# Key-value sums of the linear attention as plain float32 matmuls in four 32-column strips

## The reference, cut to what matters

```python
k = (key @ Wk.T + bk), v = (value @ Wv.T + bv)          # split into 16 heads of 16
k_prime = relu(einsum('bhnd,fd->bhnf', k, Wkf)) * attention_mask[:, None, :, None]
kv = einsum('bhnf,bhne->bhfe', k_prime, v)              # 64 x 16 for each head
qkv = einsum('bhmf,bhfe->bhme', q_prime, kv)
k_sum = sum(k_prime, axis=2)
qk_sum = einsum('bhmf,bhf->bhm', q_prime, k_sum)[..., None]
out = qkv / (qk_sum + 1e-08)
```

## Time and profile before

| | |
|---|---|
| median of 3 runs | 1415.89 us |
| profiled execution, span | 1415.0 us |
| PE busy over the span | 1280.9 us (91%) |
| weight loads busy | 1117.0 us (79%) |
| DVE / ACT / POOL busy | 1013.9 / 839.4 / 538.6 us |
| `key_value_sums`, first DMA issue to last copy | 906.02 to 1258.15 us |
| `linear_readout` | 1266.9 to about 1307.2 us |

### The profile page before, as it was taken

The page is one execution under the profiler, slowest core; times in us unless marked ns, Lnnn a source line. Parts: engine busy times, 40 slices in busy tenths (PEclk is TensorE's granted clock), DMA queues, the critical chain, the costliest instruction groups (busy, mean ns, idle before and its releaser), DMA issues. The chain is left out here.

```text
span 1415.0 us, 24244 instructions
## 1 busy us (share of the span) xinstructions
PE 1280.9 (91%) x7718; PEld 1117.0 (79%) x7718; DVE 1013.9 (72%) x2103; ACT 839.4 (59%) x1448; POOL 538.6 (38%) x551
## 2 busy tenths in 40 slices
PE   4679999999999999999996779699999999978797
PEld 3448888888888878888885768589999999965686
DVE  5857878887788887778865853488888888865533
ACT  4737667565666757666652244277777778742442
POOL 2646363644536354463522424121212121220342
PEclk9859999999999999999997889899999999989799
DMA  4031111010111101010003200211111010005000
GB/s 145 2 86 45 45 44 45 28 60 0 43 43 43 43 20 67 1 43 0 1 1 118 95 1 0 79 42 34 44 29 43 29 43 29 0 13 192 1 1 14
DMA packets 34188, 57.06 MB, mean 40 GB/s; under 512 B 2791, under 2 KB 29780, under 8 KB 33620
## 3 DMA queue, kind: packets, MB, share of 16 engines
q1 hardware_dynamic: 34132, 56.35, 12.2%
HBM read 55.89 MB, written 0.46 MB: 40 GB/s over the span
## 5 line engine op out<-in xcount | busy, mean ns | idle before, releaser
L716 POOL TENSOR_TENSOR att_sq<-att_work,att_sq 128x500 fp32r<-128x500 f32 x96 | 127.1, 1324 | 178.5 <-DVE att_sq L614 178.5
L721 POOL TENSOR_TENSOR att_k<-att_work,att_k 128x500 fp32r<-128x500 f32 x96 | 129.7, 1351 | 159.6 <-DVE att_k L622 159.6
L103 PE MATMUL att_csum<-att_pT,att_cn 125*128 125x448 f32 x384 | 155.3, 404 | 1.3 <-DVE att_pT L660 0.4
L538 ACT ACTIVATE att_pr<-att_pr,att_nmx 112x1500 f32<-112x1500 f32 (+1 forms) x96 | 108.6, 1131 | 68.1 <-DVE att_nmx L651 68.1
L105 PE MATMUL att_csum<-att_pT,att_cn 125*128 125x448 f32 x384 | 140.1, 365 | 0.0
L104 PE MATMUL att_csum<-att_pT,att_cn 125*128 125x448 f32 x384 | 139.6, 363 | 0.0
L1428 DVE SCALAR_TENSOR_TENSOR kvs_kp<-kvs_feat,kvs_kp 125x512 fp32r<-125x512 f32 x192 | 123.3, 684 | 18.4 <-ACT kvs_kp L1379 18.4
L1379 ACT ACTIVATE kvs_kp<-kvs_feat,kvs_zero 125x512 fp32r<-125x512 f32 x192 | 121.7, 685 | 23.0 <-PE kvs_feat L1312 21.4
L660 DVE TENSOR_TENSOR att_pT<-att_ring,att_pT 125x448 fp32r<-125x448 f32 x192 | 118.5, 617 | 23.1 <-ACT att_pT L554 22.8
L648 DVE TENSOR_SCALAR_CACHE_REDUCE att_pr<-att_ring 112x500 f32<-112x500 f32 x192 | 120.9, 675 | 4.4 <-PE att_ring L105 2.6
L527 ACT ACTIVATE att_work<-att_proj,att_eps 128x500 f32<-128x500 f32 x96 | 64.8, 675 | 97.0 <-PE att_proj L105 97.0
(11 more groups left out here) (256 smaller groups left out, 3486.2 us busy)
## 6 DMA issues: line engine op xcount, KB each, us to landing
att_raw_n<-in_ctx SPq DMA_DIRECT2D x16, 750.0 KB
kvs_raw<-in_ctxT SPq DMA_DIRECT2D x24, 500.0 KB, 3.6
attention_raw_t<-in_ctxT SPq DMA_DIRECT2D x7, 1500.0 KB, 6.3
w_gate<-in_gate SPq DMA_DIRECT2D x1, 2112.0 KB, 8.2
w_up<-in_up SPq DMA_DIRECT2D x1, 2112.0 KB, 12.8
qry_raw<-in_wq SPq DMA_DIRECT2D x4, 512.0 KB, 5.3
wo_raw<-in_wo SPq DMA_DIRECT2D x4, 512.0 KB, 6.3
w_down<-in_down SPq DMA_DIRECT2D x1, 2048.0 KB, 18.1
```

Of the source, the lines that this page charges most:

```text
L103: nc.tensor.matmul(out, w_lo, x_hi, start=start, stop=False, skip_group_check=True)
L716: nc.gpsimd.tensor_tensor(sq[1][:, i % 2, :], work[:, i % 2, :], sq[0][:, i % 2, :].bitcast(F32), ALU.subtract).then_inc(sq_lo, 1)
L721: nc.gpsimd.tensor_tensor(k[1][x], work[:, i % 2, :], k[0][x].bitcast(F32), ALU.subtract).then_inc(k_lo, 1)
```

## The change

The sums become plain float32 matmuls, one for each block and head (16 for each block instead of 12). The stationary operand is the 125 x 17 slice of `vs` (16 masked values of one head and the mask), the moving operand the 64 features of the same head. Head h writes to the partitions 32j to 32j+16 of one PSUM bank, j = 0 to 3, so four heads lie in four 32-column strips of the array, and the inner loop goes over the strips. `vs` and `kp` hold all 12 blocks of a batch (float32, not split), so `add` runs once a chunk over its 4 blocks, behind the first block of the next chunk.

With that, ACT and DVE share the features: ACT makes the lower half, DVE the upper half, both straight from `feat`, one instruction each for a block. The values are masked by one DVE instruction from `vals_ps` (two buffers now); the bias is no longer added there but, times the mask sum, once a batch in `read_blocks`. At the end of a batch ACT copies four strips (17 x 256 each) to SBUF, PE turns them with two 128 x 128 transposes (`turn`), and DVE writes the blocks of `kvd` with 6 instructions (`read_blocks`), in the stretch of the next batch's first chunk. `linear_readout` finds `kvd` ready: `turn_sums`, `take_low` and `diagonal` are gone, and its loop is `read`, divide, turn. `kvd` for all batches is zeroed by POOL in a block of its own ahead of `key_value_sums`.

```diff
+            def add(b, c):
+                n = b * KT + (c + 1) * TPC
+                wait(pe, v_set, n)
+                wait(pe, v_mask, n)
+                wait(pe, kp_low, n)
+                wait(pe, kp_high, n)
+                if c == 0:
+                    wait(pe, kv_taken, 4 * b)
+                for t in range(c * TPC, (c + 1) * TPC):
+                    for r in range(4):
+                        for j in range(4):
+                            h = 8 * (r // 2) + 2 * j + r % 2
+                            last = nc.tensor.matmul(sums[32 * j:32 * j + RV, r * FD:(r + 1) * FD], vs[:, t, h, :],
+                                                    kp[:, t, h * FD:(h + 1) * FD], start=(t == 0 and r == 0),
+                                                    stop=(t == KT - 1 and r == 3), skip_group_check=True)
                 last.then_inc(sums_done, 1)
+            def turn(b):
+                wait(pe, kv_taken, 4 * (b + 1))
+                wait(pe, kvd_done, 4 * b)
+                for a in range(2):
+                    last = nc.tensor.transpose(turned[:, a * 128:(a + 1) * 128], kv[:, a * 128:(a + 1) * 128], ident[:])
+                last.then_inc(kv_turned, 1)
...
+                for c, project, _ in chunks(b, last):
+                    for i in range(TPC):
+                        values(b, c * TPC + i)
+                        features(b, c * TPC + i)
+                        if i == 0:
+                            if c > 0:
+                                add(b, c - 1)
+                            elif not first:
+                                add(b - 1, KC - 1)
+                        if i in (1, 2) and project is not None:
+                            keys(*project, i - 1)
+                    if c == 0 and not first:
+                        turn(b - 1)
...
(ACT, for each block)
+                        wait(act, feat_done, 2 * (b * KT + t) + 1)
+                        nc.scalar.activation(kp[:, t, 0:512], feat[0:KP, 0, :], ACT.Relu,
+                                             bias=zero[0:KP, 0:1]).then_inc(kp_low, 1)
+                        if i in (1, 2) and project is not None:
+                            keys(*project, i - 1)
+                        if i == 2 and c == 0 and not first:
+                            take_sums(b - 1)
...
(DVE, for each block)
+                        wait(dve, v_done, n + 1)
+                        nc.vector.tensor_scalar(vs[:, t, :, 0:HE],
+                                                vals_ps[0:KP, t % 2, 0:D].rearrange("p (h e) -> p h e", e=HE),
+                                                masks[:, at_batch(b, t), 0], None, ALU.mult).then_inc(v_set, 1)
+                        wait(dve, feat_done, 2 * n + 2)
+                        nc.vector.tensor_scalar(kp[:, t, 512:1024], feat[0:KP, 1, :], 0.0, None,
+                                                ALU.max).then_inc(kp_high, 1)
+                        if i in (1, 2) and project is not None:
+                            keys(*project, i - 1)
+                    if c == 0 and not first:
+                        read_blocks(b - 1)
```

## The result

| | before | after |
|---|---|---|
| median | 1416.09 us (4 runs) | **1378.51 us** (4 runs, 1376.74 to 1382.43) |
| profiled execution, span | 1415.0 us | 1376.4 us |
| PE busy | 1280.9 us (91%) | 1218.5 us (89%) |
| a batch of the key-value sums | 42.17 us | 37.93 us |
| `key_value_sums`, from start to last write | 352.1 us | 320.2 us |

What follows compares the result with a forecast made beforehand. PE was taken to bound the key-value sums. From 1415.0 us, +13.0 (sums), +3.3 (ahead), +2.3 (behind), -4.5 (readout) and +1.2 (projection clock) gave 1430.3, forecast as a median of 1431 us; range 1390 to 1516.

Steps and rivals of the forecast that it cites:

- What bounds the kernel: Key-value sums: PE sets the pace, 42.17 us a batch; freeing ACT or DVE alone gives nothing.
- The new `add`: Key-value sums: 32 pairs of weight load and matmul a block take 0.91 us, against 1.01 before.
- starts stay in program order: In `add`: a head's second pass covers only the next head's first pass, giving 0.91 us a block.
- The three bounds: Cost of `add` a block: 1.76 us one strip after another, 0.91 partly overlapped, 0.44 with four strips at once.
- rival 2: In `add`: four strips run at once, 0.44 us a block, 45 us less, so 1386 us; chance 0.12.
- The second argument for 0.91: In `add`: issuing load and matmul takes 0.03 us a pair, so 32 pairs take 0.96 us a block.
- The estimate from TensorE: Matmul & The Clock Gate: In `add`: a documented 2.38 times for three column tiles would give 0.74 us a block and 1415 us.
- The change of tile width: Around a chunk's run of adds: 0.10 us each way, 0.2 us a chunk.
- The waits: Key-value sums: PE waits 0.85 us for DVE's features in two chunks, loses 2.1 at `turn`; seven batches +12.4 us.
- Rival 3: Key-value sums: waits smaller than followed; 1403 us without any, 1417 with half; chance 0.07.
- The +0.6 for the first batch: Key-value sums: the first batch, which has no `turn`, was to cost 0.6 us more than before.
- Ahead of the stage: Before the key-value sums: POOL zeroing `kvd` 2.2 us plus a block boundary 1.1, together +3.3 us.

Runs made afterwards that it cites:

- e1: The changed kernel with all heads' sums matmuls written to one strip instead of four, same number and shape of matmuls: 1506.03 us.
- e2: The changed kernel with heads alternating between two strips instead of four, same number and shape of matmuls: 1426.72 us.
- the repeat: A second profiled execution of the changed kernel, with nothing edited; its readout took 38.6 us against 34.4 in the first.
- e10: The changed kernel with four passes (two heads) of a strip in a row before the next strip, instead of two: 1382.47 us.
- e7: The changed kernel with keys projected one block earlier, and ACT's copies, PE's turn and DVE's `read_blocks` moved later: 1402.99 us.

## Why the prediction was wrong, point by point

- **What bounds the kernel.** Right, with a limit: a chunk of PE's own instructions now takes 4 x 0.71 + 4 x 0.95 + 2 x 1.36 + 2.11 = 11.47 us instead of 13.58, 6.3 us less a batch, of which 4.24 arrive. The other 2.1 went into waits, which were 1.4 us a batch and are 3.5 now.
- **The new `add`.** This step failed, and with it the forecast, in one clause: "starts stay in program order". A lone pass has the price that was forecast (0.0559 us measured in one strip, 0.055 forecast), but held passes are overtaken by those for other strips. Taken 0.91 us a block, measured 0.44. With the width change on both sides a chunk's adds were forecast at 4 x 0.91 + 0.2 = 3.84 us and took 2.11 (1.91, and 0.10 each in the blocks beside them): 24 runs x 1.73 = 41.5 us of the miss of 52.5. The three bounds were right, and each now has a kernel that shows it (e1; e2, at just the pace that I had taken; after). The choice among them rested on "needs no pace that the rows don't show". The shortest step in the earlier trace rows was one between matmuls of a single 98-column tile, with no second strip beside it, a case that cannot show the overlap. It was evidence for nothing, and 0.12 for rival 2 against 0.46 followed from it.
- **The second argument for 0.91**, an issue step of 0.03 us a pair, was wrong too: load and matmul are issued at 0.014 us a pair or faster.
- **The estimate from TensorE: Matmul & The Clock Gate** (the Trainium skill, Measured speedup vs the span model: 2.38 for three column tiles). The trace shows 4.0 for four tiles of 64 float32 columns, so the estimate of 0.74 us a block was too dear. It lay nearer than my 0.91, but it too would have left the kernel's time as it was (1415 us).
- **The change of tile width.** Forecast 0.2 us a chunk. Right: the features ahead of the adds take 1047.39 - 1046.36 = 1.03 instead of 0.95, and the values behind them 0.82 instead of 0.71.
- **The waits.** Right in place, cause and nearly in size. Block 0's features: 0.85 forecast, 0.76 measured (0.20 ahead of the first half, which should have started at 1057.79, and 0.56 ahead of the second). `turn`: 2.1 forecast with the turning, 1.85 measured (1.66 of wait, 0.19 for the turn, not 0.35). Rival 3 is out. Together 3.4 us a batch instead of 3.8: 3 us of the miss. The +0.6 for the first batch was a slip: without the turn's 2.1 the forecast's own batch is 41.8, which is 0.3 less than 42.17.
- **`keys`.** Not in the forecast: each half costs 1.36 instead of 1.43, with no 98-column tile ahead of it. 46 x 0.07 = 3 us.
- **Ahead of the stage.** +3.3 forecast, +2.3 measured. DVE, idle for 1.61 us ahead of its first memset in the earlier trace rows, is now idle for 3.91:

```profile
903.77 1.91 POOL L1670 MEMSET linear_kvd<- 128x2176 f32 x1 [16.49 <-POOLq L82]
...
906.28 0.27 DVE L1441 MEMSET kvs_kv<- 128x256 f32 x1 [3.91 <-PEq L1667]
```

- **Behind the stage.** +2.3 forecast, +2.4 measured.
- **Readout.** The loop, 16.0 us before, was forecast at 11.5 and takes 10.8: from the first read at 1251.43 to the copy at 1262.20, 1.20 us a batch, 0.95 for a read and 0.25 for the output's turn with both changes of width, where I had 1.3. The +1.2 for the projection at the low clock came in the repeat (6.24 us) and not in the first profile (4.67); the later fall of the clock was not in the forecast. Of the 4.2 us by which the repeat's readout is longer, 1.6 stand in the projection and 2.6 behind it.

```profile
1251.43 1.84 PE L1546 MATMUL lin_out_ps<-linear_kvd,lin_qf 128*56 128x34 f32 x32 [0.72 <-ACT lin_qf L1580]
...
1262.20 1.16 DVE L1598 COPY lin_attT<-lin_q_ps 128x448 f32<-128x448 f32 x2 [0.55 <-PE lin_q_ps L1553]
```

The miss, 1431 - 1378.5 = 52.5 us, is then: adds 41.5, keys 3, waits 3, ahead of the stage 1, readout and projection 2; the last 2 are within what unchanged phases differ by. One term carried it. The range (1390 to 1516) left out rival 2's full price, though no row spoke against it but the one that could not show it.

## What to carry to other kernels

Small stationary operands in the four 32-column strips run four at once, if the inner loop changes strip at least every four passes; a float32 matmul counts as two. When work is taken off the engine that sets the pace, look at which queues had lived on that pause. Moving their items as a whole gave nothing here in three orders. Cutting some of them into parts of 0.4 to 0.8 us, with the keys on either side of the adds, gave 16 us; which of the two did it is open. And where the trace has no row for the very thing that decides, take the bounds as the forecast; don't choose between them by a row in which the effect could not appear.

## What was not expected of the hardware

- A matmul for a busy 32-column strip is overtaken by later matmuls and loads for other strips; one streams and about three wait for each strip (in e10 four strips start within 0.040 us, past nine held matmuls), and then everything behind them stops (0.051 us a pair with 32 in a row). A strip of the array and its PSUM partitions go together here, so no run tells at which of the two a matmul waits.
- The mean step between matmuls of four strips is 0.0139 us, each with a weight load of 17 columns, and four strips reach 4.0 times the pace of one.
- PE's granted clock fell to 0.54 in the stretch behind a wait of 1.83 us inside a busy stage (e7), and that stretch cost 1.5 us more than at the full clock; in the kernel after, with waits of 1.50 us, the stage stayed at 1.00.
